# Gated delta-rule layer on one core: layer-norm statistics, last convolution blocks and layer-norm application at other places of VectorE's order

## The chip, the cores and the metric

The kernel runs on 1 core of one Trainium2 chip. The metric is the device time of one execution in microseconds, the median of several runs. The core has TensorE (PE, matrix products into PSUM), VectorE (DVE), ScalarE (ACT), GpSimd (POOL) and SyncE (SP, which here only issues DMAs). Each engine works through its own instructions in program order; what one needs from another is waited for at a semaphore.

## What is computed

The input x is 2 sequences of 4096 rows with 512 channels. The output is x plus an attention branch plus a feed-forward branch, both fed by the layer norm of x:

```python
xn = _layernorm(x, axis=-1)
x = x + attn(xn) + ffn(xn)
# attn
q, k, v = silu(causal_depthwise_conv(xn @ w, 4 taps))    # 16 heads, DK = 16, DV = 32
beta = sigmoid(xn @ b_w.T + b_bias + beta_bias) * 2.0
g = -exp(A_log) * softplus(xn @ a_w.T + dt_bias)
S = S * exp(g_t); delta = (v_t - k_t @ S) * b_t; S = S + outer(k_t, delta); o_t = q_t @ S
o = rmsnorm(o) * silu(gate) @ o_w.T
# ffn: weights are 4-bit with a scale for each 128 inputs, I = 1408
h = silu(gate) * up; y = h @ w_down.T; y / sqrt(mean(y*y) + 1e-6)
```

## The kernel before

**Tiles.** A tile is 128 rows of both sequences (NB = 2, index b), so there are 32 tiles. The recurrence is done in chunks of 32 rows (NC = 4 chunks to a tile, index c): within a chunk with a triangular solve, from chunk to chunk with a state S. The work is a software pipeline. A step handles a tile n (projections, convolution, feed-forward, and the solve of its chunks) and beside it the tile t before it (states and output of its recurrence), and prepares the layer norm of the tile after n. There are 33 steps: the first has no t, steps 2 to 31 have all three (30 steps, called full steps here), step 32 has no next tile, and the last has no n. The loop over the full steps is a hardware loop; the others are written out.

**Order.** Every engine has a function for one step (`pe_step`, `dve_step`, `act_step`, `pool_step`, `sp_step`) whose order is written out by hand. No planner is at work. `hold` is a wait with a semaphore increment behind it.

**VectorE's step, as far as the change goes.** It copies the halo and forms z; then convolution blocks 0 and 1 (`conv(0)`, L877; a block is 128 channels, and a call does two blocks, three taps each, alternating between the blocks), the small operations on g and beta, blocks 2 and 3, `keep_rows(0)` (L939) and sums of squares (L945), blocks 4 and 5, the same for b = 1. Then come four state updates `state(0..3)`: for each b a masked copy out of PSUM (L915) and two updates of S (L921). Between them stand `coefficients` and `products(0)` (L378) after `state(0)`, and `products(1)` after `state(1)`. After `state(2)` the statistics of the next tile (`layer_norm_stats`, L841 to L844), after `state(3)` its application (`layer_norm_apply`, L849) and blocks 6 and 7 (L877), then the halo copy (L1039). Behind them are 22 units of the feed-forward, three updates each (`unit(u)`, L893), a product for each pair of units (`hidden(m)`, L905), after unit 2 and before unit 3 the products of the Gram matrices (L987, L988) and sums (L1049), and `result(0)`, `result(1)` (L929) after `hidden(6)` and `hidden(8)`.

**TensorE's step.** `y_times_s(c)` (L1253) reads the state of chunk c, so that for each b it waits for `state_done` of chunk c - 1; `k_times_u(c)` (L1271) makes what `state(c)` takes from PSUM bank 7. Between them stand projections and gate products (L1235) as filling. Then `p_times_u` (L1300), units 0 to 4 (L1153, L1154) with the Gram products (L1354), units 5 to 21 with the down projection (L1166) and the output projection (L1376), the transposes of the next tile's normed rows (L1110) and the last down products. The first half of unit u waits for the first update of unit u - 2, its second half for the third update.

**ScalarE** scales the first part of every unit out of PSUM (L613) before VectorE's three updates. Ahead of unit 2 it copies the output rows of the recurrence (L771), which wait for the last `p_times_u`.

**GpSimd's step**: `split_x` (L442), g's expansions (L453 to L469), `keys_for_R` (L378), `layer_norm_scale` (L519, L521), `rest_of_x` (L448, the difference xl of 128x1024), `next_tile` (L477, waits for the last state), `keys_for_state` (L378), `gated_and_scaled` (L533 to L543) and the triangular solve (`solve`, 62 small products and differences, L511 and L515), then the feed-forward scale (L525, L527). `layer_norm_scale` stands behind a wait for the statistics:

```python
            if n:
                split_x(eng, n)
                expanded_g(eng, t, n)
                masked_g(eng, t, n)
                keys_for_R(eng, t, n)
                if more:
                    layer_norm_scale(eng, n.next())
                rest_of_x(eng, n)
                next_tile(eng, t, n)
                keys_for_state(eng, t, n)
```

Of the kernel before, what the change touches and what calls it, by code (L numbers as in the profile page):

```python
# [91 lines left out]
def build(nc, A, out):  # L92
# [4 lines left out]
    with ExitStack() as ctx:  # L97
# [4 lines left out]
        def signal(name, per):  # L102
            return Signal(ctx.enter_context(nc.semaphore("s_" + name)), per)
# [151 lines left out]
        taps_part = signal("taps_part", 16)  # L255
# [74 lines left out]
        def hold(eng, sem, value):  # L330

            eng.wait_ge(sem, value)
            eng.sem_inc(carrier.sem, 1)
# [43 lines left out]
        def put(eng, dst, src, coef):  # L377
            return eng.tensor_tensor(dst, src, bc(coef, DK), ALU.mult)  # L378

        def rows(b):  # L380
            return qk_rows[:, b, :].rearrange("p (h d) -> p h d", d=DK)
# [456 lines left out]
        def layer_norm_stats(eng, m):  # L838
            eng.wait_ge(*x_loaded.at(m, 16 * NB))
            for b in range(NB):  # L840
                eng.bn_stats(st[:, b, :], xt[:, b, :]).then_inc(stats_part.sem, 1)  # L841
            hold(eng, *stats_part.at(m, NB))
            eng.bn_aggr(mv[:, 0, :], st[:, 0, :]).then_inc(mean_part.sem, 1)
            eng.bn_aggr(mv[:, 1, :], st[:, 1, :]).then_inc(mean_done.sem, 1)  # L844

        def layer_norm_apply(eng, m):
            eng.wait_ge(*rst_done.at(m, 2))
            for b in range(NB):
                eng.tensor_scalar(xt[:, b, :], xt[:, b, :], mv[:, b, 0:1], rst[:, b:b + 1], ALU.subtract,  # L849
                                  ALU.mult).then_inc(xn_done.sem, 1)  # L850
# [12 lines left out]
                                     op0=ALU.bitwise_and, op1=ALU.bitwise_or).then_inc(f8_done.sem, 1)  # L863

        def dve_step(eng, t, n, more):
            def conv(m):

                if not n:
                    return
                for k in range(1, TAPS):  # L870
                    for mm in (m, m + 1):
                        if k == 1:
                            eng.wait_ge(*tap0_done.at(n, mm + 1))
                        elif mm == m:
                            eng.wait_ge(*taps_part.at(n, 2 * m + 2 * (k - 1)))
                        acc = qkv[:, mm, :].rearrange("p (b t) -> p b t", b=NB)
                        eng.scalar_tensor_tensor(out=acc, in0=cin[:, mm, :, k:k + P], scalar=cw[:, mm, k:k + 1], in1=acc,  # L877
                                                 op0=ALU.mult, op1=ALU.add).then_inc(
                            (taps_done if k == TAPS - 1 else taps_part).sem, 1)

            def unit(u):

                if not n:
                    return
                m = u // 2
                eng.wait_ge(*fa_scaled.at(n, u + 1))
                for k in range(1, KB):
                    if k == 2:
                        eng.wait_ge(*gu_out.at(n, 2 * u + 2))
                        eng.wait_ge(*fa_second.at(n, u + 1))  # L890
                    elif k == 3:
                        eng.wait_ge(*fa_third.at(n, u + 1))
                    eng.scalar_tensor_tensor(out=fa[:, u % 4, :], in0=PS[:, bank(u, k // 2), k % 2 * NB * P:][:, 0:NB * P],  # L893
                                             scalar=sc[:, u % 2, KB * m + k:KB * m + k + 1], in1=fa[:, u % 4, :],
                                             op0=ALU.mult, op1=ALU.add).then_inc(
                        (fa_second, fa_third, fa_done)[k - 1].sem, 1)

            def hidden(m):
                if not n:
                    return  # L900
                eng.wait_ge(*sg_done.at(n, m + 1))
                eng.wait_ge(*fa_done.at(n, 2 * m + 2))
                if m == 0:
                    eng.wait_ge(*halo_out.at(n, 1))
                eng.tensor_tensor(inner[:, m, :], fa[:, (2 * m + 1) % 4, :], sg[:, m % 2, :], ALU.mult).then_inc(h_done.sem, 1)  # L905

            def state(c):
                if not t:
                    return
                for b in range(NB):  # L910
                    i = NB * c + b + 1
                    eng.wait_ge(*ku_out.at(t, c + 1))
                    if c + b == 0:
                        eng.wait_ge(*exs_moved.at(t, 1))
                    eng.tensor_tensor(tmp[:, :, :], PS[:, 7, b * NHALF * PV:(b + 1) * NHALF * PV].rearrange("p (f n) -> p f n", f=NHALF),  # L915
                                      bdmask[:, :].unsqueeze(1).broadcast_to([P, NHALF, PV]),
                                      ALU.mult).then_inc(ku_masked.sem, 1)
                    eng.wait_ge(*ku_masked.at(t, i))
                    for f in range(NHALF):
                        k = f * NC + c  # L920
                        eng.scalar_tensor_tensor(out=S[:, (c + 1) % NC, b, f, :], in0=S[:, c, b, f, :],  # L921
                                                 scalar=exs[:, b, k:k + 1], in1=tmp[:, f, :], op0=ALU.mult,
                                                 op1=ALU.add).then_inc(
                            (state_done if f == NHALF - 1 else state_part).sem, 1)
                    eng.wait_ge(*state_done.at(t, i))

            def result(b):
                eng.wait_ge(*wo_out.at(t, b + 1))
                eng.tensor_tensor(obuf[:, b, :], obuf[:, b, :], PS[:, 6 + b, :], ALU.add).then_inc(attn_added.sem, 1)  # L929

            def keep_rows(b):

                if not n:
                    return
                eng.wait_ge(*qk_turned.at(n, b + 1))
                eng.wait_ge(*qksq_done.at(n, b + 1))
                if t and b == 0:
                    eng.wait_ge(*t_written.at(t, 16))
                eng.tensor_copy(qk_rows[:, b, :], PS[:, 6 + b, :]).then_inc(qk_kept.sem, 1)  # L939

            def sums_of_squares(b):
                if not n:
                    return
                eng.wait_ge(*qksq_done.at(n, b + 1))
                eng.tensor_reduce(ss[:, b, :], sqk[:, b, :].rearrange("p (h d) -> p h d", d=DK), AX.X,  # L945
                                  ALU.add).then_inc(ss_done.sem, 1)
# [14 lines left out]
            def products(b):  # L961
                if not n:
                    return
                eng.wait_ge(*qk_kept.at(n, b + 1))
                if t and b == 0:
                    eng.wait_ge(*a_written.at(t, 16 * NB))
                if b == 0:
                    eng.wait_ge(*coef_done.at(n, 5))
                put(eng, kqn[:, b, :].rearrange("p (h d) -> p h d", d=DK), rows(b), cn[:, b, :]).then_inc(qk_part.sem, 1)
                put(eng, kbq[:, b, 0:C // 2].rearrange("p (h d) -> p h d", d=DK), rows(b)[:, H:, :],  # L970
                    ckb[:, b, :]).then_inc(qk_part.sem, 1)
                put(eng, kbq[:, b, C // 2:].rearrange("p (h d) -> p h d", d=DK), rows(b)[:, 0:H, :],
                    cqg[:, b, :]).then_inc(qk_done.sem, 1)
# [18 lines left out]
            if n:  # L992
# [7 lines left out]
                eng.tensor_scalar(zz[:, :, :], z[:, :, :], -1.0, None, ALU.mult).then_inc(zneg_done.sem, 1)  # L1000
                eng.wait_ge(*zneg_done.at(n, 1))
                eng.tensor_tensor(zz[:, :, 0:H], z[:, :, 0:H], zz[:, :, 0:H], ALU.min).then_inc(zabs_done.sem, 1)
            conv(0)
            if n:
                eng.wait_ge(*lnz_done.at(n, 1))
                eng.scalar_tensor_tensor(out=g[:, :, :], in0=z[:, :, 0:H], scalar=0.0, in1=lnz[:, :, :], op0=ALU.max,
# [8 lines left out]
                eng.tensor_scalar(g[:, :, :], g[:, :, :], G_FLOOR, None, ALU.max).then_inc(g_done.sem, 1)  # L1015
                eng.wait_ge(*beta_part.at(n, 2))
                eng.tensor_scalar(bet[:, :, :], bet[:, :, :], 2.0, None, ALU.mult).then_inc(beta_part.sem, 1)
            conv(2)
            keep_rows(0)
            sums_of_squares(0)  # L1020
            conv(4)
            keep_rows(1)
            sums_of_squares(1)

# [3 lines left out]
            products(0)  # L1028
            state(1)
            products(1)  # L1030
            state(2)
            if n and more:
                layer_norm_stats(eng, n.next())
            state(3)
            if n and more:
                layer_norm_apply(eng, n.next())
            conv(6)
            if n:
                eng.tensor_copy(halo[:, :, :, :], cin[:, :, :, P:]).then_inc(halo_out.sem, 1)  # L1039

# [20 lines left out]
            for m in range(2, FM):  # L1061
                unit(2 * m)
                unit(2 * m + 1)
                hidden(m)
                if t and m in (6, 8):
                    result((m - 6) // 2)
            eng.wait_ge(*res_loaded.at(n, 16 * NB))
# [492 lines left out]
```

## Time and profile before

| | |
|---|---|
| median of 3 runs | 3336.32 us (3335.82 to 3341.81) |
| the profiled execution: its time, its span | 3332.51 us, 3330.7 us |
| mean granted TensorE clock | 0.988 |
| busy share of the span: PE, DVE, ACT, POOL | 94%, 72%, 50%, 58% |
| span of one full step | about 100.8 us |

All times are microseconds from the span's start unless a duration is meant. A row of the order in time gives the start, the duration, the engine (PE is TensorE's products, SPq the DMA queue of SyncE), the line of the code, the operation, out<-in, the shapes and xN for N instructions in a row; in brackets is the idle time of the engine ahead of it and what ended it. The step shown starts at 1447.90.

### The profile page before, as it was taken

Reading aid. Unit: us, or ns where it says so; the run is one execution under the profiler, and the core shown is the slowest. Engines: PE = TensorE matmul, PEld = TensorE weight load, DVE = VectorE, ACT = ScalarE, POOL = GpSimd, SP = SyncE. Lnnn points to the kernel's source line nnn. Section 1 sums busy time; section 2 is a strip of 40 time slices with the busy share of each in tenths; the row PEclk is TensorE's granted clock in tenths of the full one; section 3 lists DMA queues with packets and bytes.
Section 4 is the critical chain, followed back from the end, with each engine's and each line's share of the span. In section 5 each row is a group of like instructions: output and inputs, shape, how many; then the busy total and the mean of one; then the engine's idle time right before and its main releaser. Section 6 shows DMA issues by size and latency. Waiting matters only on the chain.

```text
span 3330.7 us, 118645 instructions
## 1 busy us (share of the span) xinstructions
PE 3142.1 (94%) x45632; PEld 2252.9 (68%) x45632; DVE 2390.6 (72%) x5408; ACT 1667.4 (50%) x3306; POOL 1918.8 (58%) x2865
## 2 busy tenths in 40 slices
PE   5999999999999999999999999999999999999995
PEld 4666766766666766666767767667667666767663
DVE  7677776777776777777777767777767777767772
ACT  3544554544554545554445545445545455544452
POOL 4566555666555665556665556665556655556652
PEclk8999999999999999999999999999999999999996
DMA  3111111111111111111111111111111111111111
GB/s 112 39 46 27 37 43 33 46 45 28 34 43 36 46 37 27 43 37 42 46 27 37 43 33 46 46 27 37 43 33 46 40 28 39 42 37 46 34 25 30
DMA packets 318318, 132.08 MB, mean 40 GB/s; under 512 B 277089, under 2 KB 278881, under 8 KB 317793
## 3 DMA queue, kind: packets, MB, share of 16 engines
q1 hardware_dynamic: 313824, 119.26, 14.3%
q8 instruction: 383, 6.28, 0.8%
q10 hardware_dynamic: 4096, 6.42, 0.5%
q14 instruction: 15, 0.11, 0.0%
HBM read 75.30 MB, written 50.33 MB: 38 GB/s over the span
## 4 chain that ended last, share of the span: by engine, by line
PE 77%; DVE 12%; issue 6%; POOL 2%; ACT 1%; ACTq 1%; DMA 1%; DVEq 0%; SPq 0%; POOLq 0%
PE PS L1166 17%; PE PS L1122 13%; PE PS L1153 8%; PE PS L1235 7%; PE PS L1154 7%; PE PS L1376 6%; DVE arena L893 4%; PE PS L1221 3%; PE PS L1300 2%; PE PS L1253 2%; DVE arena L378 2%; PE PS L1271 2%; PE PS L1391 2%; DVE arena L988 1%; PE PS L1178 1%
## 5 line engine op out<-in xcount | busy, mean ns | idle before, releaser
L893 DVE SCALAR_TENSOR_TENSOR arena<-PS,sc,arena 128x256 f32<-128x256 f32 x2112 | 1001.0, 482 | 253.0 <-ACT arena L613 152.2
L1153 PE MATMUL PS<-xh,wgu 128*128 128x256 f32 x2816 | 871.6, 341 | 35.9 <-DVE arena L893 35.4
L613 ACT ACTIVATE arena<-PS,sc 128x256 f32<-128x256 f32 x704 | 330.0, 474 | 759.0 <-PE PS L1154 700.3
L1154 PE MATMUL PS<-xl,wgu 128*128 128x256 f32 x2816 | 698.8, 282 | 0.0
L1166 PE MATMUL PS<-wdn,inner 128*128 128x512 f32 x1408 | 650.7, 592 | 0.0
L1153 PEld LDWEIGHTS PS<-xh,wgu 128*128 128x128 f32 x2816 | 531.2, 189 | 155.8 <-issue 84.2
L511 POOL TENSOR_TENSOR work<-arena 128x31 f32<-128x31 f32 (+15 forms) x992 | 511.9, 516 | 137.5 <-DMA arena<-scr_a 62.3
L515 POOL TENSOR_TENSOR arena<-arena,work 128x31 f32<-128x31 f32 (+15 forms) x992 | 542.1, 546 | 77.7
L1154 PEld LDWEIGHTS PS<-xl,wgu 128*128 128x128 f32 x2816 | 530.4, 188 | 83.2 <-issue 83.2
L1122 PE MATMUL PS<-xnT,wqkv 128*128 128x256 f32 x2048 | 485.6, 388 | 25.2 <-ACT inner L593 15.4
L1122 PEld LDWEIGHTS PS<-xnT,wqkv 128*128 128x128 f32 x2048 | 383.6, 192 | 93.1 <-ACT inner L593 16.4
L877 DVE SCALAR_TENSOR_TENSOR qkv<-inner,cw,qkv 128x256 f32<-128x256 f32 x768 | 398.8, 557 | 55.9 <-ACT qkv L600 46.7
L1166 PEld LDWEIGHTS PS<-wdn,inner 128*128 128x128 f32 x1408 | 245.5, 189 | 199.8 <-issue 199.4
L1235 PE MATMUL PS<-wg,xnT 128*128 128x512 f32 x512 | 264.8, 621 | 0.0
L1376 PE MATMUL PS<-wo,arena 128*128 128x512 f32 x512 | 242.0, 596 | 0.0
L378 POOL TENSOR_TENSOR R<-arena,ckg 128x256 f32<-128x256 f32 x64 | 57.3, 913 | 314.1 <-DVE ckt L959 314.1
L632 ACT ACTIVATE ub<-PS 32x512 f32<-32x512 f32 x256 | 136.7, 580 | 202.2 <-PE PS L1253 197.6
L905 DVE TENSOR_TENSOR inner<-arena,sg 128x256 f32<-128x256 f32 x352 | 203.4, 585 | 30.5 <-DVE arena L893 0.5
L624 ACT ACTIVATE sg<-arena 128x256 f32<-128x256 f32 x352 | 145.2, 413 | 154.1 <-DVE arena L893 153.8
L915 DVE TENSOR_TENSOR tmp<-PS,bdmask 128x128 f32<-128x128 f32 x256 | 74.1, 289 | 206.2 <-PE PS L1271 201.8
L533 POOL TENSOR_TENSOR arena<-arena 128x512 f32<-128x512 f32 x64 | 80.4, 1278 | 226.3 <-ACT qkv L776 226.3
L1071 DVE SCALAR_TENSOR_TENSOR obuf<-PS,yr,obuf 128x512 f32<-128x512 f32 x64 | 45.1, 745 | 217.6 <-POOL yr L527 217.6
(147 smaller groups left out, 4619.2 us busy)
## 6 DMA issues: line engine op xcount, KB each, us to landing
xt<-in_x SPq DMA_DIRECT2D x64, 256.0 KB, 2.8
scr_a<-arena SPq DMA_DIRECT2D x64, 256.0 KB, 2.4
arena<-scr_a SPq DMA_DIRECT2D x256, 64.0 KB, 3.2
obuf<-in_x SPq DMA_DIRECT2D x64, 256.0 KB, 2.8
scr_t<-arena SPq DMA_DIRECT2D x32, 512.0 KB, 2.7
arena<-scr_t SPq DMA_DIRECT2D x256, 64.0 KB, 2.3
out<-obuf SPq DMA_DIRECT2D x64, 256.0 KB, 2.0
wqkv<-in_wqkv ACTq DMA_DIRECT2D x1, 2048.0 KB, 14.3
```

Of the source, the lines that this page charges most:

```text
L511: eng.tensor_tensor(pr, la[:, j, j + 1:].unsqueeze(1).broadcast_to([P, w, r]), bc(lt[:, 0:w, j], r), ALU.mult).then_inc(solve_part.sem, 1)
L515: eng.tensor_tensor(tail, tail, pr, ALU.subtract).then_inc((t_done if j == CH - 2 else solve_part).sem, 1)
L613: eng.activation(fa[:, u % 4, :], PS[:, bank(u, 0), 0:NB * P], ACT.Copy, scale=sc[:, u % 2, KB * m:KB * m + 1]).then_inc(fa_scaled.sem, 1)
L877: eng.scalar_tensor_tensor(out=acc, in0=cin[:, mm, :, k:k + P], scalar=cw[:, mm, k:k + 1], in1=acc, op0=ALU.mult, op1=ALU.add).then_inc((t ...
L893: eng.scalar_tensor_tensor(out=fa[:, u % 4, :], in0=PS[:, bank(u, k // 2), k % 2 * NB * P:][:, 0:NB * P], scalar=sc[:, u % 2, KB * m + k:K ...
L905: eng.tensor_tensor(inner[:, m, :], fa[:, (2 * m + 1) % 4, :], sg[:, m % 2, :], ALU.mult).then_inc(h_done.sem, 1)
L1122: ins = eng.matmul(PS[:, proj_bank(m), 0:NB * P], wqkv[:, kb, m * P:(m + 1) * P], xnT[:, kb, :], start=(kb == 0), stop=(kb == KB - 1))
L1153: eng.matmul(o, w, xh[:, k, :], start=True, stop=False)
L1154: ins = eng.matmul(o, w, xl[:, k, :], start=False, stop=True)
L1166: ins = eng.matmul(PS[:, b, :], inner[:, m, b * P:(b + 1) * P], wdn[:, m, :], start=(m == 0), stop=(m == FM - 1))
L1235: ins = eng.matmul(PS[:, 4 + b, :], xnT[:, kb, b * P:(b + 1) * P], wg[:, kb, :], start=(kb == 0), stop=(kb == KB - 1))
L1376: ins = eng.matmul(PS[:, 6 + b, :], oT[b][:, kb, :], wo[:, kb, :], start=(kb == 0), stop=(kb == KB - 1))
```

## The change

The statistics of the next tile go from behind `state(2)` to behind the convolution of blocks 2 and 3. Blocks 6 and 7 are no longer done together behind `state(3)`: block 6 stands between `products(1)` and `state(2)`, block 7 between `state(2)` and `state(3)`. `conv` takes its blocks as arguments; with one block its three taps follow one another. The application of the layer norm goes from behind `state(3)` to behind `hidden(7)`. GpSimd's, ScalarE's, TensorE's and SyncE's orders stay as they are, and so do the operations.

```diff
-            def conv(m):
+            def conv(*blocks):
 
                 if not n:
                     return
                 for k in range(1, TAPS):
-                    for mm in (m, m + 1):
+                    for mm in blocks:
                         if k == 1:
                             eng.wait_ge(*tap0_done.at(n, mm + 1))
-                        elif mm == m:
-                            eng.wait_ge(*taps_part.at(n, 2 * m + 2 * (k - 1)))
+                        elif mm == blocks[0]:
+                            eng.wait_ge(*taps_part.at(n, 2 * mm + len(blocks) * (k - 1)))
...
-            conv(2)
+            conv(2, 3)
+            if n and more:
+                layer_norm_stats(eng, n.next())
             keep_rows(0)
             sums_of_squares(0)
-            conv(4)
+            conv(4, 5)
             keep_rows(1)
             sums_of_squares(1)
...
             products(0)
             state(1)
             products(1)
+            conv(6)
             state(2)
-            if n and more:
-                layer_norm_stats(eng, n.next())
+            conv(7)
             state(3)
-            if n and more:
-                layer_norm_apply(eng, n.next())
-            conv(6)
             if n:
                 eng.tensor_copy(halo[:, :, :, :], cin[:, :, :, P:]).then_inc(halo_out.sem, 1)
...
                 hidden(m)
+                if more and m == 7:
+                    layer_norm_apply(eng, n.next())
                 if t and m in (6, 8):
                     result((m - 6) // 2)
```

## Rows read from the trace of the kernel before

**Rows 1.** The page's chain that ended last, shares of the span by engine.
```profile
PE 77%; DVE 12%; issue 6%; POOL 2%; ACT 1%; ACTq 1%; DMA 1%; DVEq 0%; SPq 0%; POOLq 0%
```

**Rows 2.** Busy time by stretch: start:end, length, busy by engine (instructions), clock, DMA share, GB/s.
```profile
1492.90:1504.30 11.40, 9.04 (x177) 7.60 (x178) 10.61 (x22) 8.70 (x16) 9.23 (x6) 1.00 0.35 76
1504.30:1548.70 44.40, 44.40 (x215) 29.77 (x214) 30.57 (x62) 14.62 (x32) 37.10 (x68) 1.00 0.13 41
```

**Rows 3.** The chain in order of time: start, duration, what.
```profile
1492.64 0.48 ACT arena L613
1493.15 0.50 DVE arena L893
```

**Rows 4.** VectorE in order of time, the full step shown, up to the units.
```profile
1460.87 0.69 DVE L939 COPY arena<-PS 128x512 f32<-128x512 f32 x1 [3.12 <-ACT arena L650]
...
1469.25 0.48 DVE L921 SCALAR_TENSOR_TENSOR S<-S,exs,tmp 128x64 f32<-128x64 f32 x2
...
1473.68 0.48 DVE L921 SCALAR_TENSOR_TENSOR S<-S,exs,tmp 128x64 f32<-128x64 f32 x2
...
1477.38 0.29 DVE L915 TENSOR_TENSOR tmp<-PS,bdmask 128x128 f32<-128x128 f32 x1 [1.82 <-PE PS L1271]
...
1479.15 1.29 DVE L841 BATCH_NORM_STATS2 st<-xt 128x6 f32<-128x512 f32 x2
...
1482.70 2.06 DVE L921 SCALAR_TENSOR_TENSOR S<-S,exs,tmp 128x64 f32<-128x64 f32 x2
...
1485.64 1.00 DVE L849 TENSOR_SCALAR xt<-xt,mv,rst 128x512 f32<-128x512 f32 x2
...
1490.01 4.74 DVE L893 SCALAR_TENSOR_TENSOR arena<-PS,sc,arena 128x256 f32<-128x256 f32 x9
```

**Rows 5.** GpSimd in order of time, same step.
```profile
1470.54 1.78 POOL L378 TENSOR_TENSOR R<-arena,ckg 128x256 f32<-128x256 f32 x2 [9.87 <-DVE ckt L959]
1481.04 0.22 POOL L519 TENSOR_SCALAR rst<-mv 128x2 f32<-128x2 f32 x1 [8.72 <-DVE mv L844]
...
1482.14 2.35 POOL L448 TENSOR_TENSOR xl<-xnT,xh 128x1024 fp32r<-128x1024 f32 x1
...
1497.72 5.44 POOL L538 TENSOR_TENSOR ro<-ro,mhalf 128x32 f32<-128x32 f32 x1 [0.18 <-POOL ro L535]
```

**Rows 6.** TensorE in order of time: the products with the state.
```profile
1469.88 0.43 PE L1253 MATMUL PS<-S,YT 32*32 32x64 f32 x16 [0.27 <-DVE S L921]
...
1474.97 0.65 PE L1253 MATMUL PS<-S,YT 32*32 32x64 f32 x32
...
1479.61 0.65 PE L1253 MATMUL PS<-S,YT 32*32 32x64 f32 x32
```

**Rows 7.** The last tile's step, which has no statistics: GpSimd, in order of time.
```profile
3188.06 2.53 POOL L448 TENSOR_TENSOR xl<-xnT,xh 128x1024 fp32r<-128x1024 f32 x1
```

**Rows 8.** The same step: VectorE's state update of chunk 1, b = 0.
```profile
3188.62 2.25 DVE L921 SCALAR_TENSOR_TENSOR S<-S,exs,tmp 128x64 f32<-128x64 f32 x2
```

**Rows 9.** The same step: TensorE's product with the state of chunk 2, b = 1.
```profile
3191.86 0.43 PE L1253 MATMUL PS<-S,YT 32*32 32x64 f32 x16 [0.42 <-DVE S L921]
```

**Rows 10.** VectorE beside the long GpSimd operation, and among the late units.
```profile
1499.89 0.75 DVE L905 TENSOR_TENSOR inner<-arena,sg 128x256 f32<-128x256 f32 x2
...
1530.33 1.59 DVE L893 SCALAR_TENSOR_TENSOR arena<-PS,sc,arena 128x256 f32<-128x256 f32 x3 [1.00 <-ACT arena L613]
...
1533.25 3.08 DVE L893 SCALAR_TENSOR_TENSOR arena<-PS,sc,arena 128x256 f32<-128x256 f32 x6
```

**Rows 11.** TensorE: first product of unit 21's second half.
```profile
1536.87 0.28 PE L1153 MATMUL PS<-xh,wgu 128*128 128x256 f32 x1
```

**Rows 12.** SyncE: the load of the next tile's x, issued.
```profile
1452.37 0.91 SPq L389 DMA_DIRECT2D xt<-in_x  x2
```

**Rows 13.** The page's DMA issues: size of one, us from issue to landing.
```profile
xt<-in_x SPq DMA_DIRECT2D x64, 256.0 KB, 2.8
```

**Rows 14.** GpSimd among the late units: one product of the solve.
```profile
1526.52 0.74 POOL L515 TENSOR_TENSOR arena<-arena,work 128x256 f32<-128x256 f32 x1
```

More of the change, by code:

```diff
@@ L1002, in dve_step @@
                 eng.tensor_tensor(zz[:, :, 0:H], z[:, :, 0:H], zz[:, :, 0:H], ALU.min).then_inc(zabs_done.sem, 1)
-            conv(0)
+            conv(0, 1)
             if n:
```

## The prediction

> **What bounds the kernel now.** I read the page's chain first: three quarters of the time to the end runs through TensorE and an eighth through VectorE [rows 1], so the question is in which stretch VectorE is the one waited for. The busy time by stretch answers it for one full step. From 1504.30 to 1548.70 TensorE has no idle time at all; from 1492.90 to 1504.30 it is busy for 9.04 of 11.40 us while VectorE is busy for 10.61 [rows 2]. VectorE bounds only that short stretch. Then the chain in order of time says where the stretch begins: ScalarE's scale of unit 2 (1492.64, 0.48 long), and VectorE's update of unit 2 from 1493.15 on [rows 3]. That scale stands behind ScalarE's copies of the recurrence's output, which wait for TensorE's last `p_times_u`. So TensorE's own order sets the start of the stretch, and whether VectorE is late for it decides what this change can gain. The last view is VectorE's and GpSimd's order in the middle of the step [rows 4, 5], since that is where the change moves work.
>
> **What it frees on VectorE.** Between `state(3)` and unit 0, from 1485.64 to 1490.01, stand the application (1.00 us), blocks 6 and 7 and the halo's copy [rows 4]; all but the copy go, more than 4 us. What does that open? In the step shown the nine updates of units 0 to 2 take 4.74 us from 1490.01, and three take 1.59 [rows 4, 10], so VectorE came free for unit 2 at 1490.01 + 4.74 - 1.59 = 1493.16; the scale it needs ended at 1492.64 + 0.48 = 1493.12 [rows 3]. They arrive together. With VectorE early by any amount unit 2 can start 0.04 us sooner and no more, since the scale comes out of TensorE's order. Steps differ among each other by tenths, so I take 0 and as the far end -0.2 us a step. The work from unit 2 to unit 5 is unchanged, and so is TensorE's wait for it. The freed time lies under a wait for ScalarE.
>
> **Statistics, earlier.** Ahead of `keep_rows(0)` VectorE idles for 3.12 us, from 1457.75 [rows 4]. From the start of the statistics at 1479.15 to GpSimd's first operation on them at 1481.04 are 1.89 us, the aggregations and the handing over included [rows 4, 5]; they fit. Their wait is for the load of x: issued from 1452.37 for 0.91 us [rows 12], landing 2.8 us after issue [rows 13], so the later one is there at about 1452.9 + 2.8 = 1455.7, 2 us before it is asked for. Queued behind the wait would be `keep_rows(0)` and through it `decay_sums` on TensorE. Cost 0; if x came 3.4 us later, that cover would be gone.
>
> **Blocks 6 and 7 alone.** Done alone, a block's three taps follow one another like the three updates of a unit, 1.59 us [rows 10]. Block 6 starts at 1477.38 - 1.82 = 1475.56 and would end at 1477.15, before `state(2)` gets its input at 1477.38 [rows 4]. Block 7 falls into the idle time before `state(3)`, which grows by the statistics that leave it. Taken by itself, cost 0.
>
> **What the statistics' move releases on GpSimd.** This is the term that decides. Today `layer_norm_scale` waits 8.72 us for the statistics, and `rest_of_x`, queued behind it, starts at 1482.14 [rows 5]. With the statistics there at 1457.75 + 1.89 = 1459.64, GpSimd runs on from `keys_for_R`, which ends at 1470.54 + 1.78 = 1472.32. From L519 to the start of L448 it takes 1482.14 - 1481.04 = 1.10 us, so xl would start at 1473.42 and, at 2.35 us, end at 1475.77 [rows 5]. What stands next to it now? Where xl runs today VectorE's two updates of S take 2.06 us [rows 4], from 1482.70 to 1484.76, 0.27 us beyond xl's end at 1484.49; elsewhere the pair takes 0.48. The first of the pair does not move until xl is through. Today that hits `state(3)`, which nobody on TensorE is waiting for soon. Moved, xl meets `state(1)`: the pair for b = 1 starts at 1473.68, 0.26 us behind xl's new start, and would end at 1475.77 + 0.27 = 1476.04 instead of 1474.16, 1.88 us later.
>
> Who waits: `y_times_s(2)`, whose 32 products start at 1474.97, the second 16 of them about 0.3 us later, at 1475.3 [rows 6]. From the end of `state(0)` at 1469.25 + 0.48 = 1469.73 to the products that it releases at 1469.88 are 0.15 us [rows 4, 6]. So the second half starts at 1476.04 + 0.15 = 1476.19: TensorE is 0.9 us later. Everything of chunk 2 follows from there, and `products(1)` and block 6 end at 1476.04 + 1.40 + 1.59 = 1479.03 (1.40 from 1474.16 to the idle time's start at 1475.56), then `state(2)` in 1.65 us (from 1477.38 to just before 1479.15, an estimate) at 1480.7, while `y_times_s(3)`, moved by 0.9 from 1479.61, wants b = 1 at 1480.8 [rows 4, 6]. It just fits; 0.1 to 0.3 us more are possible. Behind that TensorE is in its own order up to unit 2, so the whole step moves by 0.9.
>
> The trace has this case once. The last tile has no statistics, and there xl follows `keys_for_R` directly, at 3188.06 [rows 7]; `state(1)`'s first pair takes 2.25 us [rows 8] and TensorE idles 0.42 us before the second half of `y_times_s(2)` [rows 9]. It is the same collision with xl 1.1 us earlier, so that b = 0 is caught and b = 1 follows late. It makes the mechanism all but certain; as part of the delay there lies ahead of b = 0, 0.42 is a lower bound of its size.
>
> **The application among the late units.** 1.00 us for both halves [rows 4]. Behind `hidden(7)` VectorE has 1.00 us of idle time before unit 17, at 1530.33 [rows 10]. Unit 21's second half starts on TensorE at 1536.87 [rows 11] and needs unit 19's third update, done at 1533.25 + 3.08 = 1536.33 [rows 10]: 0.54 us in hand. So 1.5 us can be absorbed and the cost is 0; what GpSimd's solve could do to it is rival 4.
>
> **The sum.** 30 full steps have both a state and statistics. 30 x (0.9 + 0 + 0 + 0 + 0) = 27 us, on the profiled execution's 3332.5 us: 3359.5. The median of the runs lies 3.8 us above that execution, so 3363; the 0.04 us a step that VectorE's early arrival gives makes it 3362.
>
> **The rivals.** (1) *GpSimd's power operation holds VectorE up too.* Between `keys_for_R` and xl stands the small power operation L521, from about 1472.7, which reads two operands. If it too held VectorE up, the updates for b = 0 would slip behind it, xl would come in between, and both halves of `state(1)` would be late: 1475.77 + 0.27 + 0.80 (the masked copy and pair for b = 1) + 0.15 = 1477.0 against 1475.3, 1.7 us a step, 3336 + 51 = 3387. Against it: beside GpSimd's 5.44 us power operation [rows 5] VectorE's two products of two operands took 0.75 us [rows 10], undisturbed.
>
> The Trainium skill (SBUF — State Buffer, Who interferes with whom) says that a VectorE instruction with two SBUF inputs and a GpSimd one that reads SBUF exclude each other, and that the one that starts first has the shared port for its whole instruction. The pair of 2.06 us beside xl agrees; the 0.75 us beside the power operation does not, if "whole" is meant for every operation. Read to the letter the rule gives this rival's time.
>
> (2) *Same.* xl comes a little later than 1473.42 and VectorE's pair goes first, the collision falls on `products(1)` and block 6, and TensorE's later slack takes it. Then only the tie at unit 2 is left, 0 to -0.2 us a step: 3330 to 3338. For it: 0.26 us decide which instruction is first. Against it: whichever operation of VectorE is caught then, it has two operands as well, and `state(2)` would end near 1480.9, again behind TensorE's 1479.61 + 0.3.
>
> (3) *Faster.* VectorE's freed 4 us do reach the stretch that it bounds, because unit 2's scale is not what starts it. All of TensorE's idle time there, 11.40 - 9.04 = 2.4 us [rows 2], would go in each of 31 steps: 3336 - 73 = 3263, or a part of it. It decides if VectorE is found idle before unit 2 and TensorE is nevertheless earlier. Against it: the tie of rows 3 and 4, and the last tile's step, where VectorE is idle early and the stretch is still there.
>
> (4) *The application in the way.* Among the late units GpSimd's solve is always at work, in operations of up to 0.74 us [rows 14]. If each half of the application waits one out, 1.00 becomes 2.5; the idle 1.00 and the 0.54 in hand take 1.5 of it, and up to 0.9 us a step are left, 27 us; half of it if the wait is half an operation on the mean. Alone that gives 3336 to 3363, with the forecast up to 3389. Against it: in the one place where the trace shows them, right behind `state(3)`, the two take 1.00 together [rows 4].
>
> **How the numbers follow.** The forecast 0.60, rival 1 0.12, rival 2 0.14, rival 3 0.06, rival 4 (instead of the forecast, or on top of it) 0.08. A measurement of this kernel can tell 0.2% from no change, 6.7 us. Slower by more holds the forecast, rivals 1 and 4: 0.80. Within 0.2% is rival 2 without its far end, 0.13, and faster is rival 3 with a little of rival 2, 0.07. The forecast's own range, 0.6 to 1.2 us a step, is 3354 to 3372, and with 0.13 us a step either way for the small terms 3350 to 3376. For 8 in 10 it reaches over most of rivals 2, 4 and 1: 3335 to 3386.
>
> **What would show it.** Of the changed kernel: POOL L448 starts about 9 us earlier, directly behind the layer-norm scale, and `state(3)`'s updates take 0.48 each pair again while a pair of `state(1)` takes near 2 us. TensorE idles 0.5 to 1 us more before L1253's second half for chunk 2, on VectorE's S. VectorE idles about 1.5 us before unit 0 and near 0.5 before unit 2, with the start of unit 2 later within the step by 0.9, not earlier. The full step is 101.7 us long. The forecast is wrong if xl starts elsewhere, if the slow pair is not in `state(1)`, or if TensorE's wait at the products with the state stays at 0.27 us.

## The result and the profile after

The changed kernel takes 3370.6 us (median of 3 runs, 3364.85 to 3373.02) against 3336.32 before: ratio 1.0089, 95% interval 1.0075 to 1.0103. It is slower by 34 us. The profiled execution has a span of 3368.8 us against 3330.7, 38.1 us more, or 38.1 / 30 = 1.27 us for each full step; the granted clock is 0.989, as before.

TensorE's waits in the whole execution, kernel after (who waited for whom: us in total, times, longest):

```profile
PE PS L1154 <- DVE arena L893: 36.3, 99, 0.5
PE PS L1254 <- DVE S L921: 32.9, 58, 0.9
PE PS L1355 <- DVE arena L988: 26.3, 32, 1.4
```

(The edits shift the line numbers a little: the products with the state are L1253 to L1256, the updates of S L921 to L923, depending on the kernel.) The kernel before has 35.4, 8.3 and 28.7 us in these places (units, products with the state, Gram products). One has grown: the products with the state wait 24.6 us longer for VectorE's update of S. The units' wait, which the 4 us freed on VectorE could have shortened, is the same.

The middle of one full step after, in order of time. `state(0)` begins at 2403.03 (at 1468.09 in the step of rows 4 to 6). VectorE:

```profile
2407.78 0.49 DVE L921 SCALAR_TENSOR_TENSOR S<-S,exs,tmp 128x64 f32<-128x64 f32 x2
2408.31 0.29 DVE L915 TENSOR_TENSOR tmp<-PS,bdmask 128x128 f32<-128x128 f32 x1
2408.64 2.48 DVE L921 SCALAR_TENSOR_TENSOR S<-S,exs,tmp 128x64 f32<-128x64 f32 x2
...
2412.43 1.52 DVE L877 SCALAR_TENSOR_TENSOR qkv<-inner,cw,qkv 128x256 f32<-128x256 f32 x3
...
2418.74 0.48 DVE L921 SCALAR_TENSOR_TENSOR S<-S,exs,tmp 128x64 f32<-128x64 f32 x2
...
2424.86 1.59 DVE L893 SCALAR_TENSOR_TENSOR arena<-PS,sc,arena 128x256 f32<-128x256 f32 x3 [4.57 <-ACT arena L613]
2426.75 1.59 DVE L893 SCALAR_TENSOR_TENSOR arena<-PS,sc,arena 128x256 f32<-128x256 f32 x3 [0.30 <-ACT arena L613]
2428.89 1.59 DVE L893 SCALAR_TENSOR_TENSOR arena<-PS,sc,arena 128x256 f32<-128x256 f32 x3 [0.55 <-ACT arena L613]
```

GpSimd, same step:

```profile
2405.48 1.78 POOL L378 TENSOR_TENSOR R<-arena,ckg 128x256 f32<-128x256 f32 x2 [9.81 <-DVE ckt L959]
2407.35 0.28 POOL L519 TENSOR_SCALAR rst<-mv 128x2 f32<-128x2 f32 x1
2407.81 0.71 POOL L521 TENSOR_TENSOR rst<-rst,mhalf 128x2 f32<-128x2 f32 x1 [0.18 <-POOL rst L519]
2408.50 2.34 POOL L448 TENSOR_TENSOR xl<-xnT,xh 128x1024 fp32r<-128x1024 f32 x1
```

TensorE, same step:

```profile
2409.90 0.69 PE L1254 MATMUL PS<-S,YT 32*32 32x64 f32 x16
2411.26 0.43 PE L1254 MATMUL PS<-S,YT 32*32 32x64 f32 x16 [0.67 <-DVE S L921]
```

The three engines' rows have to be read side by side. GpSimd no longer waits for the statistics ahead of xl (8.72 us in rows 5), and xl starts at 2408.50. The S pair for b = 1 of chunk 1 starts 0.14 us behind it and takes 2.48 us instead of 0.48. Its end at 2411.12 is 0.28 behind xl's end at 2410.84, and 0.14 us after it TensorE starts the second half of `y_times_s(2)`, having idled for 0.67. The pair of `state(3)`, 2.06 us in rows 4, is back at 0.48. VectorE's freed time is where it says "ACT arena L613": 4.57 us before unit 0, 0.30 and 0.55 before the next two.

Two smaller points of the same trace. The pair for b = 0 started at 2407.78, 0.03 us ahead of the power operation L521; its second update ran inside L521's 0.71 us, and the pair took 0.49: that operation does not hold VectorE up. And the stretch that VectorE bounds has kept its size. Taken from the start of the first Gram products, as in rows 2, TensorE is busy for 9.30 of 11.40 us there, and without idle time behind it (before, 9.04 of 11.40):

```profile
2428.64:2440.04 11.40, 9.30 (x177) 7.54 (x178) 10.42 (x21) 8.60 (x16) 9.23 (x6) 1.00 0.36 76
2440.04:2479.20 39.16, 39.16 (x187) 25.70 (x186) 30.03 (x61) 10.94 (x26) 33.39 (x59) 1.00 0.12 33
```

### The profile page after: what moved, and what is told of

Same layout as the page of the kernel before. It is cut to its first block, busy times and chain, and to the rows that moved or that the text cites. A ratio compares the mean times of both kernels' runs of the same rounds, so it can differ in the third digit from the quotient of the medians.

```text
span 3368.8 us, 118674 instructions
## 1 busy us (share of the span) xinstructions
PE 3155.1 (94%) x45632; PEld 2257.3 (67%) x45632; DVE 2406.4 (71%) x5408; ACT 1672.9 (50%) x3306; POOL 1906.8 (57%) x2865
## 4 chain that ended last, share of the span: by engine, by line
PE 69%; DVE 11%; issue 9%; POOL 6%; DMA 2%; SPq 1%; ACT 1%; ACTq 1%; DVEq 0%; POOLq 0%
PE PS L1167 15%; PE PS L1123 12%; PE PS L1154 7%; PE PS L1155 6%; PE PS L1236 6%; PE PS L1377 6%; DVE arena L893 4%; POOL arena L515 3%; PE PS L1222 3%; POOL work L511 3%; PE PS L1301 3%; PE PS L1272 2%; PE PS L1254 1%; PE PS L1392 1%; DVE S L921 1%
## 5 line engine op out<-in xcount | busy, mean ns | idle before, releaser
L613 ACT ACTIVATE arena<-PS,sc 128x256 f32<-128x256 f32 x704 | 331.0, 476 | 749.2 <-PE PS L1155 691.2
L877 DVE SCALAR_TENSOR_TENSOR qkv<-inner,cw,qkv 128x256 f32<-128x256 f32 x768 | 387.4, 532 | 59.0 <-ACT qkv L600 43.9
L921 DVE SCALAR_TENSOR_TENSOR S<-S,exs,tmp 128x64 f32<-128x64 f32 x512 | 185.2, 403 | 9.0
```

The source lines that it names most:

```text
L613: eng.activation(fa[:, u % 4, :], PS[:, bank(u, 0), 0:NB * P], ACT.Copy, scale=sc[:, u % 2, KB * m:KB * m + 1]).then_inc(fa_scaled.sem, 1)
```

## The experiments

The theory: the loss comes from xl, which the early statistics release into `state(1)`. Rivals: the early statistics themselves; blocks 6 and 7 between the states; the late application. The kernel before took 3327 to 3328 us beside these runs, on their chips, so they are told by ratio; expectations in us are from a base of 3336. Names with b_ start from the kernel before, those with a_ from the changed one; c_ is described where it stands.

### One part at a time

**Statistics alone.**

```diff
             conv(2)
+            if n and more:
+                layer_norm_stats(eng, n.next())
             keep_rows(0)
...
             state(2)
-            if n and more:
-                layer_norm_stats(eng, n.next())
             state(3)
```

> The kernel before with only the statistics moved to behind blocks 2 and 3; blocks 6 and 7 stay together behind state(3), and so does the application. Theory (the statistics' move releases xl on GpSimd, which then holds the state update of chunk 1): nearly the whole loss is here, 1.1 to 1.3 us in each of 30 steps, 3336 + 33 to 39 = 3369 to 3375; the state pair for b = 1 of state(1) takes near 2.5 us and TensorE's products with the state of chunk 2 wait for it. Rival (block 6 ahead of state(2) delays the state chain): no more than the 0.9 of the forecast, 3363 or less. Rival (late application): 3336, same.

Measured: 1.0089 (1.0075 to 1.0102), the same ratio as the whole change. On the base of 3336 that is 3366: 3 us below what the theory gave and 3 above what the rival of block 6 allowed, so it is the next two runs, not this number, that settle the rivals. The S pair, then the products that wait for it:

```profile
2095.75 2.48 DVE L921 SCALAR_TENSOR_TENSOR S<-S,exs,tmp 128x64 f32<-128x64 f32 x2
```
```profile
2098.38 0.43 PE L1253 MATMUL PS<-S,YT 32*32 32x64 f32 x16 [0.93 <-DVE S L921]
```

**Blocks 6 and 7 alone.**

```diff
             products(1)
+            conv(6)
             state(2)
             if n and more:
                 layer_norm_stats(eng, n.next())
+            conv(7)
             state(3)
             if n and more:
                 layer_norm_apply(eng, n.next())
-            conv(6)
```

(`conv` itself is changed here as in the whole change.)

> The kernel before with only blocks 6 and 7 taken apart: block 6 ahead of state(2), block 7 behind the statistics and ahead of state(3), application behind state(3). Theory: same, 3330 to 3340; VectorE comes earlier to unit 0 and then waits for ScalarE's scale, so nothing is gained. Rival (the blocks delay the state chain): slower by 0.2 to 0.4 us a step, 3342 to 3348. Rival (VectorE's earlier arrival helps the stretch that it bounds): faster, down to 3263.

Measured: 0.9987 (0.9978 to 0.9996), a little faster, 3323.7 us. VectorE is idle ahead of the first three units:

```profile
2087.73 1.59 DVE L893 SCALAR_TENSOR_TENSOR arena<-PS,sc,arena 128x256 f32<-128x256 f32 x3 [1.36 <-ACT arena L613]
2089.51 1.59 DVE L893 SCALAR_TENSOR_TENSOR arena<-PS,sc,arena 128x256 f32<-128x256 f32 x3 [0.19 <-ACT arena L613]
2091.66 1.59 DVE L893 SCALAR_TENSOR_TENSOR arena<-PS,sc,arena 128x256 f32<-128x256 f32 x3 [0.55 <-ACT arena L613]
```

It gains 4 us, 0.14 us in each of 31 steps (0.04 to 0.24 by the interval), where the faster rival had up to 2.4. The place of the blocks is no part of the loss. Only a small part of the gain is the tie at unit 2: in the kernel before VectorE starts that unit 0.06 us behind the end of ScalarE's scale (mean of 30 steps; it is late in 5 of them, by up to 0.2), here 0.03 in every step. So an idle VectorE is worth about 0.02 us a step there. Where the rest comes from is not shown: the scale itself ends 0.14 us earlier in this trace, but it does so by as much in that of b_apply_late, which gains nothing clear of noise.

**The application alone.**

```diff
             state(3)
-            if n and more:
-                layer_norm_apply(eng, n.next())
             conv(6)
...
                 hidden(m)
+                if more and m == 7:
+                    layer_norm_apply(eng, n.next())
```

> The kernel before with only the application moved behind hidden(7). Theory: same, 3332 to 3339, its 1.0 us lies in VectorE's idle time before units 16 and 17. Rival (the solve's operations hold the application up and the late units wait): slower by up to 0.9 us a step, up to 3363.

Measured: 0.9996 (0.9987 to 1.0005), same. Rival 4 had its mechanism half right. In the changed kernel the two halves take 1.74 us beside the solve instead of 1.00, and the six updates behind them 3.22 instead of 3.08:

```profile
2462.79 1.74 DVE L849 TENSOR_SCALAR xt<-xt,mv,rst 128x512 f32<-128x512 f32 x2
2464.46 3.22 DVE L893 SCALAR_TENSOR_TENSOR arena<-PS,sc,arena 128x256 f32<-128x256 f32 x6
```

The idle time and the slack behind them take it all: from TensorE's start of unit 17 to the next tile's first products it takes 16.34 us on the mean in the kernel before, 16.35 in b_apply_late and 16.34 in the changed kernel.

### Where xl runs

**Kept off until `state(2)` is done.** The changed kernel, GpSimd's step:

```diff
                 if more:
                     layer_norm_scale(eng, n.next())
+                if t:
+                    hold(eng, *state_done.at(t, 6))
                 rest_of_x(eng, n)
```

> The changed kernel with one more wait on GpSimd: xl waits for state(2) of the tile before. It runs then beside block 7 and nothing that TensorE waits for. Theory: all of the loss comes back, 3330 to 3338, state(1)'s pairs take 0.48 us each again, a tap of block 7 takes near 2 us. Rival (the loss is in the blocks between the states or in the late application): the kernel stays at 3365 or above.

Measured: 0.9992 (0.9983 to 1.0001). With early statistics, split blocks and late application all in place, one wait that lets xl meet block 7 instead of `state(1)` makes the whole loss go away:

```profile
2081.79 2.45 POOL L448 TENSOR_TENSOR xl<-xnT,xh 128x1024 fp32r<-128x1024 f32 x1 [5.82 <-DVE S L923]
```
```profile
2076.08 0.48 DVE L923 SCALAR_TENSOR_TENSOR S<-S,exs,tmp 128x64 f32<-128x64 f32 x2
...
2081.54 2.98 DVE L879 SCALAR_TENSOR_TENSOR qkv<-inner,cw,qkv 128x256 f32<-128x256 f32 x2
```

The collision is as large as before: two taps of block 7 take 2.98 us. Only nobody on TensorE is waiting behind it.

**xl early, VectorE untouched.** The kernel before, with two calls of GpSimd's step swapped:

```diff
-                if more:
-                    layer_norm_scale(eng, n.next())
                 rest_of_x(eng, n)
+                if more:
+                    layer_norm_scale(eng, n.next())
```

> The kernel before, VectorE's order untouched; on GpSimd alone xl is put ahead of the layer-norm scale, so that it no longer waits for the statistics. Theory (what costs is when xl runs, not where the statistics stand): slower like the change, 0.9 to 1.2 us in each of 30 steps, ratio 1.008 to 1.011; both halves of state(1) late as in the last tile's step of the kernel before. Rival (the early statistics themselves cost, through keep_rows or the load of x): same as before.

Measured: 1.0060 (1.0047 to 1.0074): slower without any edit on VectorE, though by less than expected. xl starts right behind `keys_for_R` here and catches the pair for b = 0; b = 1 follows at once, and the second half of the products waits 0.33 us after a first wait of 0.20:

```profile
2086.43 2.53 POOL L448 TENSOR_TENSOR xl<-xnT,xh 128x1024 fp32r<-128x1024 f32 x1
```
```profile
2086.68 0.28 DVE L915 TENSOR_TENSOR tmp<-PS,bdmask 128x128 f32<-128x128 f32 x1
2086.99 2.25 DVE L921 SCALAR_TENSOR_TENSOR S<-S,exs,tmp 128x64 f32<-128x64 f32 x2
```
```profile
2089.38 0.51 PE L1253 MATMUL PS<-S,YT 32*32 32x64 f32 x16 [0.20 <-DVE S L921]
2090.22 0.43 PE L1253 MATMUL PS<-S,YT 32*32 32x64 f32 x16 [0.33 <-DVE S L921]
```

`state(1)` ends 0.24 us earlier than in the changed kernel (table below); the early start makes up for having both halves late.

**Kept off until `state(1)` is done.** As above, with 4 instead of 6: xl meets `products(1)`.

> The changed kernel with one more wait on GpSimd: xl waits for state(1) instead of state(2). It meets products(1) and block 6 instead of state(1). My reckoning from the trace: products(1) and block 6 end 2 us later, state(2) ends at about 13.0 us after the start of state(0) instead of 10.95 and TensorE's products with the state of chunk 3, which want it at 11.8, are 1.0 to 1.4 us late: ratio 1.008 to 1.012. Rival (only a collision with state(1) reaches TensorE, later slack takes the rest): same, 0.999 to 1.002.

Measured: 1.0074 (1.0060 to 1.0088), just under what was expected and against its rival. A product of 0.42 us takes 2.57, block 6 and `state(2)` follow late, and it is now the products with the state of chunk 3 that wait:

```profile
2093.23 2.57 DVE L378 TENSOR_TENSOR arena<-arena,ckb 128x256 f32<-128x256 f32 x1
```
```profile
2098.44 0.43 PE L1256 MATMUL PS<-S,YT 32*32 32x64 f32 x16 [0.35 <-DVE S L923]
2099.28 0.43 PE L1256 MATMUL PS<-S,YT 32*32 32x64 f32 x16 [0.41 <-DVE S L923]
```

So it is not a property of `state(1)`. In both places tried between `state(0)` and `state(2)` the 2 us on VectorE reach TensorE; beside block 7, behind `state(2)`, they don't.

### How long xl is

**Half of it.** In the changed kernel, with the second half of xl left out:

```diff
-            eng.tensor_tensor(xl[:, :, :], xnT[:, :, :], xh[:, :, :].bitcast(F32), ALU.subtract).then_inc(xl_done.sem, 1)
+            eng.tensor_tensor(xl[:, 0:2, :], xnT[:, 0:2, :], xh[:, 0:2, :].bitcast(F32), ALU.subtract).then_inc(xl_done.sem, 1)
```

> The changed kernel with xl's operation cut to its first half (128x512): the other half of xl is left out, so the feed-forward is computed from a wrong remainder for half of the channels; everything else runs as before. If the loss is the time by which xl's end outlasts TensorE's slack of 0.8 us, the slow pair ends 1.17 us sooner, at 6.9 us after the start of state(0) instead of 8.1, and TensorE does not wait: ratio 0.999 to 1.001. Rival (a constant cost for each collision, or the early statistics): 1.004 to 1.009.

Measured: 0.9998 (0.9989 to 1.0007). The same as before, though the pair is still held up and takes 1.40 us in all:

```profile
2077.09 1.26 POOL L448 TENSOR_TENSOR xl<-xnT,xh 128x512 fp32r<-128x512 f32 x1
```
```profile
2077.22 1.40 DVE L921 SCALAR_TENSOR_TENSOR S<-S,exs,tmp 128x64 f32<-128x64 f32 x2
```

**Three quarters of it.** The same with 0:3.

> The same with three quarters of xl (128x768), a quarter left out. The slow pair ends 0.58 us sooner than in the changed kernel, at 7.5 us after the start of state(0); TensorE's products with the state of chunk 2 are late by 0.5 us in each of 30 steps: ratio 1.004 to 1.006, with up to 0.002 more if the lumps in TensorE's issue add what they add in the changed kernel. Rival (constant cost): 1.009.

Measured: 1.0048 (1.0032 to 1.0063), in the middle of what was expected. The pair takes 1.94 us.

**Four pieces.** All of xl, in four operations of 128x256, with the semaphore counting to 4 (its declaration and its two waits are not shown):

```diff
-            eng.tensor_tensor(xl[:, :, :], xnT[:, :, :], xh[:, :, :].bitcast(F32), ALU.subtract).then_inc(xl_done.sem, 1)
+            for k in range(KB):
+                eng.tensor_tensor(xl[:, k, :], xnT[:, k, :], xh[:, k, :].bitcast(F32), ALU.subtract).then_inc(xl_done.sem, 1)
```

> The changed kernel with xl as four GpSimd operations of 128x256 instead of one of 128x1024; nothing else. Theory (the holder keeps the other engine out for one instruction, and the waiting one gets in behind it): a state update waits 0.6 us at most at a time, state(1) ends at about 7 instead of 8.1 us after the start of state(0), TensorE's 0.8 us of slack takes most of it: 0 to 0.4 us a step, ratio 1.000 to 1.004. Rival (GpSimd keeps VectorE out over all four, or the two share by speed): like the change, 1.009.

Measured: 1.0042 (1.0028 to 1.0056), just above what was expected. The two engines take turns, an instruction each:

```profile
2084.53 3.23 POOL L449 TENSOR_TENSOR xl<-xnT,xh 128x256 fp32r<-128x256 f32 x4
```
```profile
2084.67 1.34 DVE L922 SCALAR_TENSOR_TENSOR S<-S,exs,tmp 128x64 f32<-128x64 f32 x2
2086.05 1.12 DVE L378 TENSOR_TENSOR arena<-arena,cn 128x512 f32<-128x512 f32 x1
2087.09 0.94 DVE L378 TENSOR_TENSOR arena<-arena,ckb 128x256 f32<-128x256 f32 x1
```

The pair of `state(1)` is through soon enough (1.34), but xl now lasts longer and the next two products are held up in their turn (0.69 and 0.42 alone). The wait appears at chunk 3: 0.42 us before the second half. Pieces spread the delay, they don't remove it.

### The runs side by side

Means over the 29 full steps behind the first, in us: when `state(1)` ends, when TensorE starts the gate product right behind `y_times_s(2)`, when it starts unit 0 (these three from the start of `state(0)`), and the length of the step from its first product to the next step's. Each row is one profiled execution; the ratio is of medians.

| kernel | `state(1)` ends | after `y_times_s(2)` | unit 0 | step | ratio |
|---|---|---|---|---|---|
| before | 6.08 | 7.59 | 19.46 | 100.91 | 1 |
| a_xl_half | 7.01 | 7.59 | 19.55 | 100.90 | 0.9998 |
| a_xl_threeq | 7.55 | 8.05 | 20.00 | 101.49 | 1.0048 |
| b_xl_first | 7.85 | 8.35 | 20.28 | 101.51 | 1.0060 |
| b_stats_moved | 8.09 | 8.59 | 20.53 | 101.82 | 1.0089 |
| after | 8.09 | 8.59 | 20.67 | 102.21 | 1.0089 |
| a_xl_after_state1 | 6.09 | 7.55 | 20.41 | 101.67 | 1.0074 |
| a_xl_pieces | 6.96 | 7.53 | 20.05 | 101.34 | 1.0042 |
| a_xl_after_state2 | 6.09 | 7.57 | 19.45 | 100.72 | 0.9992 |

The first six rows are a curve with a knee. Up to about 7.09 (7.59 - 0.50) TensorE does not notice the end of `state(1)`. Beyond, the product behind `y_times_s(2)` starts 0.50 us after it, each time. The slack of the kernel before is thus 7.09 - 6.08 = 1.0 us, and xl beside `state(1)` costs 2.0.

**A try at more.** The units' stretch begins with ScalarE's scale of unit 2; in b_conv_split VectorE is there first. Put between the two copies that it stands behind:

```diff
-                for b in range(NB):
-                    eng.activation(by_pair(sq[:, b, :]), paired(1, b), ACT.Copy).then_inc(o_copied.sem, 1)
-            unit(2)
+            for b in range(NB):
+                if t:
+                    eng.activation(by_pair(sq[:, b, :]), paired(1, b), ACT.Copy).then_inc(o_copied.sem, 1)
+                if b == 0:
+                    unit(2)
```

> The kernel before with blocks 6 and 7 taken apart, and ScalarE's scale of unit 2 between its two copies of the recurrence's output instead of behind both. If that scale is what starts the stretch that VectorE bounds, VectorE starts unit 2 about 0.3 us sooner; the second copy and with it the first Gram products are 0.5 us later, which takes part of it back: 0 to 0.2 us a step better than the blocks alone, ratio 0.997 to 0.999. Rival (the Gram products' wait for the second copy weighs more): 1.000 to 1.002.

Measured: 0.9984 (0.9975 to 0.9993), 3321.4 us beside 0.9987 for the blocks alone: no difference that these runs can tell. By the traces, from the start of `state(0)`, unit 2's scale ends 0.06 us sooner in the median of the steps (0.21 in the mean, as some steps gain more) and VectorE's use of the first Gram products begins 0.17 us later (0.04 in the mean). So unit 2 is a little earlier and the Gram products behind it are not.

## Why the prediction was right

**The term that decides** was found where it is. xl starts 5.47 us after `state(0)` instead of 14.05 (8.6 us earlier, "about 9" was said), `state(3)`'s pair is back at 0.48, the slow pair is that of `state(1)`, b = 1, and TensorE waits ahead of the second half of `y_times_s(2)`. That this alone makes the loss, and nothing else that the change did, is shown from four sides: the statistics' move alone has the whole ratio, the two other edits have none of it, one wait on GpSimd takes it away, and swapping two calls on GpSimd gives 1.0060 without any edit on VectorE.

**Its size** was said to be 0.9 us a step. Measured are 34 / 30 = 1.13 between the medians, inside the forecast's 0.6 to 1.2, and 1.27 between the two profiled executions, just above it. The term that was too small is the sum for `state(1)`'s end. It said 1476.04, 7.95 after the start of `state(0)`; 8.09 was measured, because L519 starts 0.09 us behind the end of `keys_for_R`, where nothing was reckoned, and from its start to xl's are 1.15 us (L519 takes 0.28) instead of the 1.10 taken from its place before (0.22). That gives TensorE 1.00 us in the mean instead of 0.9 (8.59 against 7.59).

Another 0.2 us comes between there and unit 0 (20.67 - 19.46 = 1.21), while b_stats_moved, b_xl_first and a_xl_threeq have only 0.06 to 0.08 there. The prediction had allowed 0.1 to 0.3 us for `state(2)` being late for `y_times_s(3)`, but that is not it: `state(2)` ends at 12.48 in the mean, and the products start at 12.64, as they do in b_stats_moved. Most of it is idle time inside `p_times_u`, under "issue", in which TensorE waits for nothing that the profile shows; first after, then b_stats_moved:

```profile
PE PS L1301 <- issue: 15.4, 43, 1.8
```
```profile
PE PS L1300 <- issue: 10.7, 30, 1.5
```

The difference is 0.16 us a step. But this idle time is 12.1 us in the kernel before and 7.6 to 12.6 in the other runs, though the order of these products is the same in all of them, and the time ahead of `state(0)`, 0.1 us longer in after than before, varies among the traces by 0.2. As the ratios of after and b_stats_moved, each against its own runs of the kernel before, are both 1.0089, the extra 0.2 us may belong to the execution that was profiled and not to the change. What makes it is not settled.

**VectorE's freed time** was said to lie under a wait for ScalarE, worth 0.04 us in the step shown and at most 0.2. The mechanism holds, and by the traces of b_conv_split it is worth 0.02 us a step; of the 0.14 that its ratio gives the rest is open. How idle VectorE would be ahead of unit 0 was misjudged: about 1.5 us was said, and it is 4.57. It changed nothing in the sum.

**Statistics earlier**: done in 1.7 us, without a wait for x, and of the 3.12 us of idle time ahead of `keep_rows(0)` 1.46 are left. (By its own terms the prediction's limit for a late x is 2.0 + 3.12 - 1.89 = 3.2 us rather than 3.4.)

```profile
2392.67 1.27 DVE L841 BATCH_NORM_STATS2 st<-xt 128x6 f32<-128x512 f32 x2
2394.10 0.18 DVE L843 BATCH_NORM_AGGREGATE mv<-st 128x2 f32<-128x6 f32 x1 [0.16 <-DVE st L841]
2394.20 0.15 DVE L844 BATCH_NORM_AGGREGATE mv<-st 128x2 f32<-128x6 f32 x1
2395.81 0.69 DVE L939 COPY arena<-PS 128x512 f32<-128x512 f32 x1 [1.46 <-ACT arena L650]
```

**Blocks alone**: 1.52 us for three taps, 1.59 said.

**The rivals.** Rival 1 (the power operation holds VectorE up) did not happen: 0.49 us for the pair whose second update ran inside it. The Trainium skill (SBUF — State Buffer, Who interferes with whom) has the rule that, of a VectorE instruction with two SBUF inputs and a GpSimd one that reads SBUF, the later waits for the whole of the earlier. It agrees with all that was measured beside xl (2.25, 2.48, 2.57 and the taps of block 7) and with the turns in a_xl_pieces. It does not hold for the power operations, here as in rows 5 and 10. Rival 2 (TensorE's later slack takes it) was tried by a_xl_after_state1 and fell, by the reasoning that stood against it: 1.0074. That a collision can cost nothing is true, though: with half of xl it is there, and TensorE does not wait. Rival 3 fell with b_conv_split. Rival 4's longer application came (1.74 us), its cost did not.

## What to carry to other kernels

A wait can be a schedule: GpSimd's wait for the statistics looked like waste, and it kept an operation of 2.35 us away from the updates that TensorE was waiting for. Before moving what an engine waits for, follow what is queued behind the wait to its new time and look at which instructions of the other engine run there. And before freeing time on an engine, check what its next instruction would wait for: here VectorE and ScalarE arrived at unit 2 within 0.04 us of each other, and the time freed ahead of it bought 0.02 there.

## What the runs showed of the hardware

- An operation of GpSimd that reads SBUF and one of VectorE with two SBUF inputs kept each other out for an instruction at a time, and the one that waited went next: a pair of S updates behind xl in one piece takes 2.48 us (0.48 alone), behind four pieces 1.34, with a piece of GpSimd's ahead of each of its two. The masked copy, which has one input from PSUM, was not affected (L915: 0.28 inside xl in b_xl_first, 0.29 elsewhere).
- The one that waits does not start from nothing when the other ends: an S update ended 0.08 us after xl (0.27 to 0.29 alone), a product of 128x256 0.28 us after it in a_xl_after_state1 (0.42 alone). And GpSimd waits too: xl took 2.53 and 2.56 us where it started beside a running product of VectorE's (b_xl_first, a_xl_after_state1), and 2.34 in the changed kernel, where it did not.
- Cutting an operation has its own price on GpSimd: 128x512, 128x768 and 128x1024 take 1.26, 1.80 and 2.34 us, so 0.54 for each 256 elements and 0.18 fixed. Four pieces of 0.72 would be 2.9 by that; they took 3.23: three took 0.72 to 0.73, and the last 1.17, beside a product of 128x512 on VectorE.
- Power operations of GpSimd on small operands take long (5.44 us for 128x32, 0.71 for 128x2), but VectorE's two-input operations ran beside them at full speed (0.49 for a pair, 0.75 for two products). L521 itself took 0.83 us beside taps of block 7 in b_conv_split.
- VectorE's layer-norm application, with one tensor input of 128x512, was slowed beside GpSimd's solve: its two halves took 0.96 and 0.86 us in the changed kernel, 0.55 each behind `state(3)`.
